# Two-block convolution and attention network, batch 4: another order at the start, image 2's and 3's normalisation in other banks, head attention through diagonal matrices

## What is computed

```python
x = x + L0(gn(x))     # block 1
x = x + L1(gn(x))     # block 2
# L0: the first 48 channels: layer norm over channels at each pixel, q (16), k (16), v (48),
#     full softmax attention over the 1024 pixels; relu(concat(attended, other 144)), a 192x192 product
# L1: qkv = 192 -> 576; heads of 24 channels: attention over channels of a head (q, k normalised
#     over the pixels, times a temperature, softmax over 24), attended = attn @ v
#     conv_x = depthwise 3x3 of a 1x1 of v;  t = cp_in(attended) (32 channels)
#     channel map from t, mean(t) and a 3x3 and a dilated 7x7 convolution of t
#     spatial map from conv_x: 1x1, depthwise 3x3, gelu gate, 1x1
#     out = proj(attended * sigmoid(spatial) + conv_x * sigmoid(mean of the channel map))
```

## Time and profile before

| what | value |
|---|---|
| median of 3 runs | 359.26 us (358.64 to 360.69) |
| the profiled execution | 360.42 us |
| its span, first to last instruction | 358.4 us |
| PE / DVE / ACT / POOL busy | 312.2 / 265.2 / 167.0 / 23.3 us |
| mean granted TensorE clock | 0.965 |

### The profile page before, as it was taken

How to read it: one execution, slowest core, us unless ns; L and a number is a source line. 1 busy time by engine, 2 the same in 40 slices (tenths; PEclk the granted TensorE clock), 3 DMA queues, 4 the chain that set the end, 5 groups by cost and what they waited for, 6 DMA issues and landing times. The chain is left out here.

```text
span 358.4 us, 6337 instructions
## 1 busy us (share of the span) xinstructions
PE 312.2 (87%) x2642; PEld 148.2 (41%) x2642; DVE 265.2 (74%) x496; ACT 167.0 (47%) x288; POOL 23.3 (6%) x29
## 2 busy tenths in 40 slices
PE   0279899999999599999899999998999878897995
PEld 0146265333346334543353546444243355433431
DVE  4444765867278957779989679978967999769653
ACT  1024307664561348734832387536632774375320
POOL 2012010000002400000100110001000001100000
PEclk9999758999999969999999999999999999999999
DMA  8460000000000000210000010200000315013005
GB/s 263 153 180 2 0 0 0 2 0 3 0 3 2 0 2 16 63 25 0 2 0 3 0 34 13 59 0 2 0 2 0 114 30 135 2 34 69 2 2 176
DMA packets 6074, 12.45 MB, mean 35 GB/s; under 512 B 2078, under 2 KB 2718, under 8 KB 5918
## 3 DMA queue, kind: packets, MB, share of 16 engines
q1 hardware_dynamic: 5532, 11.97, 12.3%
q10 hardware_dynamic: 514, 0.08, 0.1%
HBM read 5.32 MB, written 3.15 MB: 24 GB/s over the span
## 5 line engine op out<-in xcount | busy, mean ns | idle before, releaser
L1639 DVE SCALAR_TENSOR_TENSOR dd<-spp,wt,dd 112x1024 f32<-112x1024 f32 x32 | 41.0, 1283 | 2.5 <-ACT dd L2214 1.7
L1628 DVE SCALAR_TENSOR_TENSOR cx<-cpA,dw2w,cx 128x1024 f32<-128x1024 f32 x32 | 40.9, 1277 | 1.9 <-ACT cx L2133 1.8
L2101 ACT ACTIVATE pT<-psA 128x1024 f32<-128x1024 f32 x24 | 24.6, 1024 | 20.2 <-PE psA L649 15.1
L658 PE MATMUL psO<-pT,vt 128*64 128x512 f32 x96 | 25.1, 612 | 0.3 <-ACT pT L2101 0.2
L1628 DVE SCALAR_TENSOR_TENSOR cx<-cpB,dw2w,cx 128x512 f32<-128x512 f32 x32 | 23.8, 744 | 0.0
L1487 DVE TENSOR_REDUCE nmp<-psA 128x2 f32<-128x1024 f32 x16 | 19.6, 1225 | 5.3 <-PE psA L629 5.1
L845 PE MATMUL psR<-up,wb 128*32 128x256 f32 (+1 forms) x336 | 20.9, 383 | 0.1
L2059 ACT ACTIVATE xa<-x,gb,gr 48x512 f32<-48x512 f32 x8 | 6.5, 811 | 24.1 <-DVE gb L1444 24.0
L649 PE MATMUL psA<-qs,ks 50*128 50x512 f32 x48 | 12.0, 496 | 4.2 <-ACT pT L2101 2.6
L1419 DVE BATCH_NORM_STATS2 st<-x 128x6 f32<-128x512 f32 x24 | 15.5, 683 | 0.2
L2458 POOL TENSOR_TENSOR gr<-gvar,mhalf 128x2 f32<-128x2 f32 x8 | 6.0, 754 | 140.7 <-DVE gvar L1438 140.7
(11 more groups left out here) (429 smaller groups left out, 691.8 us busy)
## 6 DMA issues: line engine op xcount, KB each, us to landing
up<-up SPq DMA_DIRECT2D x12, 200.0 KB, 3.1
x<-x_dram SPq DMA_DIRECT2D x4, 512.0 KB, 6.0
out_dram<-x SPq DMA_DIRECT2D x8, 256.0 KB, 2.3
wt<-params_dram SPq DMA_DIRECT2D x1, 1151.5 KB, 6.8
tp<-tp SPq DMA_DIRECT2D x8, 136.0 KB, 2.4
x<-x_dram SPq DMA_DIRECT2D x8, 128.0 KB, 4.6
out_dram<-x SPq DMA_DIRECT2D x8, 128.0 KB, 2.5
wt<-params_dram SPq DMA_DIRECT2D x1, 213.5 KB, 2.6
```

Source lines behind the costliest of these rows:

```text
L658: last = mm(s.o_ps[rows(n), :], s.vt[:, t, :], s.pT[t % 2][:, n * HB:(n + 1) * HB], start=(t == 0), stop=(t == NKT - 1))
L1628: v.scalar_tensor_tensor(acc, img, dw2w[:, blk, tap:tap + 1], acc, ALU.mult, ALU.add).then_inc(cv_s.of(c), 1)
L1639: v.scalar_tensor_tensor(acc, t.spp[:, dy:dy + HH, dx:dx + WW], par("w_spdw")[:, tap:tap + 1], acc, ALU.mult, ALU.add).then_inc(dv_s.of(c), 1)
L2101: a(s.pT[t % 2][:], s.scoreT_ps[:], ACT.Exp).then_inc(ex_s.of(b), 1)
```

## The change

It does six things.

1. SP loads image 0 ahead of the first parameters; ACT issues its small loads first; DVE makes image 0's statistics before the group matrices are spread, and `setup2_a`, which waits for the small loads, stands behind `pixel_var(0)`. DVE norms one half of image 0's 48 channels itself (`normed1_half`), ACT the other.
2. PE begins with six products of `xn`, which POOL has filled with ones (`warm_up`), a seventh after `setup_ln`; the `keep_warm` products stand at other places.
3. The norm chains of images 2 and 3 use other banks (`cen_ps`, `norm_ps`, `mean_ps`: image 2 psR and psS, image 3 psB) and own semaphores and run ahead; `q_product`, `t_product(0)`, `sp_in_a(0)` and `conv1_a(2)` get waits for it. The inverse denominators get a tile of their own, `rD`.
4. Head scores are made transposed and copied (`copy_scores`), and multiplied by a diagonal of k's inverse norms on PE (`k_scaled`), which gives them scaled and the other way round; the mask is added in the same DVE instruction. The division by the softmax sums is a product with a diagonal too (`divided_attn`), which also transposes.
5. t's weights come from the undivided exponentials: `t_head` multiplies them by `wcpT` divided by the sums (`wcs`), `t_weights` by v's weights. The product of attention by v's weights and its 384-column copy go away.
6. All five lists are in another order; `store(0)` and `store(1)` stand ahead of `shift_u(1)` and `shift_t(2)`.

```diff
-        one[0].cen_ps, one[1].cen_ps = psR[:, 0:HB], psA[:, 0:HB]
+        cen_ps = [psR[:, 0:HB], psA[:, 0:HB], psR[:, 0:HB], psB[:, 0:HB]]
+        norm_ps = [psR[:, HB:N], psO, psR[:, HB:N], psB[:, HB:N]]
+        mean_ps = [psS, psO, psS, psB[:, HB:N]]
...
+            load_x(0)
             sp.dma_start(wt[:, 0:N1], params[:, 0:N1]).then_inc(s_w1, 16)
-            load_x(0)
             load_x(1)
...
             def group_means(i, b):
-                if i == 0 and TURN1[b]:
-                    pe.wait_ge(*x2_s(b - 1, 2))
-                    pe.wait_ge(*gmm[1](b - 1, 1))
+                if i == 0 and b == 2:
+                    pe.wait_ge(*x2_s(0, 2))
+                    pe.wait_ge(*gmm[1](0, 1))
+                if i == 0 and b == 3:
+                    pe.wait_ge(*mce_s(1, 3))
+                    pe.wait_ge(*mte_s(1, 4))
...
-            def k_norm_rows(c):
+            def k_scaled(c):
                 pe.wait_ge(*dk_s(c, 2))
+                pe.wait_ge(*rk_s(c, 1))
                 for h in range(2):
-                    for j in range(2):
-                        last = mm(front.F[1][rows(j), h * CH:(h + 1) * CH], ones[0:CH, 0:SP2], front.dk[:, h, :],
-                                  start=True, stop=True)
+                    last = columns(front.F[1][:, h * CH:(h + 1) * CH], front.st[:, h * CH:h * CH + P], front.dk[:, h, :])
...
+            def t_head(c):
+                pe.wait_ge(*sm_s(c, 6))
+                for h in range(2):
+                    last = columns(front.F[0][:, h * C6:(h + 1) * C6], front.sx[:, h * CH:h * CH + P], front.wcs[:, h, :])
+                last.then_inc(uh_s.of(c), 1)
...
             def attn_weights(c):
                 pe.wait_ge(*ate_s(c, 1))
                 wv = par2("wv")
                 for h in range(2):
-                    last = columns(front.F[0][:, h * C:(h + 1) * C], front.att[:, h * CH:h * CH + P], wv[:, h, :])
-                last.then_inc(mp_s.of(c), 1)
-                for h in range(2):
...
+            def warm_up(k):
+                if k == 0:
+                    pe.wait_ge(s_fill, 1)
+                mm(psB[:, HB:N][:, 0:QB], one[0].xn[:, 0:P], one[0].xn[:, 0:QB], start=True, stop=True)
...
+            def normed1_half():
+                s, g = one[0], stats[0][0]
+                dve.wait_ge(*gmm[0](0, 4))
+                dve.wait_ge(s_mem, 3)
+                v.tensor_scalar(s.xa[SP2:SPN, :], xs[0][0:PD, 1, :], g.gr[0:PD, 0:1], g.gb[0:PD, 0:1],
+                                ALU.mult, ALU.add).then_inc(s_xa0, 1)
...
             def scaled_scores(c):
-                dve.wait_ge(*rk_s(c, 1))
+                dve.wait_ge(*kr_s(c, 1))
                 dve.wait_ge(*sm_s(c, 1))
-                dve.wait_ge(*sc_s(c, 1))
                 for h in range(2):
-                    v.scalar_tensor_tensor(front.dk[:, h, :], front.F[0][0:CH, h * CH:(h + 1) * CH], front.rq[:, h:h + 1],
-                                           front.rk[:, h, :], ALU.mult, ALU.mult).then_inc(sm_s.of(c), 1)
+                    v.scalar_tensor_tensor(front.sc[:, h, :], front.F[1][0:CH, h * CH:(h + 1) * CH], front.rq[:, h:h + 1],
+                                           par("mask"), ALU.mult, ALU.add).then_inc(sm_s.of(c), 1)
                 dve.wait_ge(*sm_s(c, 3))
-                v.tensor_tensor(front.dk[:], front.dk[:], par("mask").unsqueeze(1).broadcast_to([CH, 2, CH]),
-                                ALU.add).then_inc(sm_s.of(c), 1)
```

More of the change, by code:

```diff
@@ L1045, in _ @@
             transpose_x(0, 0)
-            transpose_x(0, 1)
             proj1_a(1)
             proj1_b(1)
+            proj1_last(1)
+            center(2)
+            transpose_x(0, 1)
             transpose_x(0, 2)
-            proj1_last(1)
+            pixel_var(2)
             gram_x(0)
+            gram_w(0)
             group_means(1, 1)
-            group_means(0, 2)
-            gram_w(0)
-            center(2)
+            rstd_rows(2)
             head_scores(0)
-            pixel_var(2)
             norms(0)
-            rstd_rows(2)
-            k_norm_rows(0)
+            q_product(2)
+            k_product(2)
+            k_scaled(0)
             sp_in_a(0)
-            q_product(2)
-            transpose_attn(0)
-            k_product(2)
+            t_head(0)
+            divided_attn(0)
+            t_weights(0)
             attn_weights(0)
-            t_weights(0)
             v_product(2)
+            score_rows(2, 0)
+            t_product(0)
             conv1_a(1)
             conv1_b(1)
-            score_rows(2, 0)
-            t_product(0)
             score_rows(2, 1)
+            ci1_product(0)
             conv1_last(1)
+            transpose_x(1, 0)
             score_rows(2, 2)
-            transpose_x(1, 0)
-            ci1_product(0)
+            ci2a(0)
+            score_rows(2, 3)
             transpose_x(1, 1)
             transpose_x(1, 2)
-            score_rows(2, 3)
-            ci2a(0)
             score_rows(2, 4)
@@ L1130, in _ @@
             proj2_last(0)
+            center(3)
+            sp_in_a(1)
+            pixel_var(3)
+            t_product(1)
             group_means(1, 2)
-            attn_weights(1)
-            group_means(0, 3)
-            sp_in_a(1)
             sp_in_b(1)
-            t_weights(1)
-            center(3)
-            t_product(1)
-            pixel_var(3)
+            rstd_rows(3)
+            ci1_product(1)
+            q_product(3)
             conv1_a(2)
             conv1_b(2)
-            rstd_rows(3)
+            ci2a(1)
             conv1_last(2)
-            ci1_product(1)
             transpose_x(2, 0)
-            ci2a(1)
+            k_product(3)
             transpose_x(2, 1)
             transpose_x(2, 2)
-            q_product(3)
-            k_product(3)
+            v_product(3)
             gram_x(2)
-            v_product(3)
             score_rows(3, 0)
-            gram_w(2)
-            score_rows(3, 1)
             ci2b(1, 0)
             ci2b(1, 1)
-            score_rows(3, 2)
+            score_rows(3, 1)
             ci2b(1, 2)
             ci2b(1, 3)
+            score_rows(3, 2)
+            ci2b(1, 4)
             score_rows(3, 3)
-            ci2b(1, 4)
+            gram_w(2)
+            score_rows(3, 4)
             ci2b(1, 5)
-            score_rows(3, 4)
+            score_rows(3, 5)
             sp_out_a(1)
             ci2b(1, 6)
-            score_rows(3, 5)
+            score_rows(3, 6)
             sp_out_b(1)
             map_mean(1)
-            score_rows(3, 6)
+            score_rows(3, 7)
             attended_a(1)
-            score_rows(3, 7)
-            attended_b(1)
             max_rows(3)
@@ L1227, in _ @@
             ci2b(2, 4)
-            k_norm_rows(3)
+            sp_out_a(2)
+            k_scaled(3)
+            sp_out_b(2)
             ci2b(2, 5)
-            ci2b(2, 6)
-            sp_in_a(3)
-            transpose_attn(3)
-            attn_weights(3)
-            t_weights(3)
-            sp_out_a(2)
+            sp_in_a(3)
+            t_head(3)
+            divided_attn(3)
+            t_weights(3)
+            attn_weights(3)
+            ci2b(2, 6)
+            map_mean(2)
             t_product(3)
-            map_mean(2)
             sp_in_b(3)
             ci1_product(3)
-            sp_out_b(2)
             attended_a(2)
@@ L1676, in _ @@
             channel_stats(0, 0, 2)
+            setup_ln()
             moments(0, 0)
-            setup2_a()
-            group_stats(0, 0)
-            group_shift(0, 0)
-            setup_qkv()
-            channel_stats(0, 1, 0)
-            channel_stats(0, 1, 1)
-            setup_marks()
-            pixel_var(0)
-            channel_stats(0, 1, 2)
-            moments(0, 1)
+            group_matrices()
+            setup_marks()
+            group_stats(0, 0)
+            channel_stats(0, 1, 0)
+            group_shift(0, 0)
+            normed1_half()
+            channel_stats(0, 1, 1)
+            setup_qkv()
+            channel_stats(0, 1, 2)
+            pixel_var(0)
+            moments(0, 1)
+            setup2_a()
             setup_weights()
-            setup2_b()
             layer_norm(0)
@@ L1741, in _ @@
             normed(0)
+            moments(0, 2)
+            channel_stats(0, 3, 0)
+            channel_stats(0, 3, 1)
+            channel_stats(0, 3, 2)
             inverse_denominators(1)
+            group_stats(0, 2)
+            group_shift(0, 2)
             conv2(0, 0)
```

578 lines of the change are left out of this document (308 added, 270 removed).

## The result

The changed kernel takes 350.63 us (median of four, 349.89 to 352.18) against 359.98 for the kernel before in the same comparison: a ratio of 0.973, 95% interval 0.9679 to 0.9782. That is 9.4 us less; 17 were forecast. The profiled execution has a span of 347.8 us, before 358.4.

The account below looks back on a forecast made before the run. PE bounds 130 to 204 us, DVE 278 to 306; loose time lay at the start, in the scores and at 98 to 130. 11 + 0 + 5 + 1 + 0 = 17 off a 358.4 span; predicted time 342.5, range 336 to 348.

Parts of the forecast that it names:

- Step 1: Start up to image 0's q product: earlier image load, statistics and norms, mostly at the high clock; -11 us.
- What I had named as a sign of being wrong: At the start: `center(0)` is held by the warm products.
- Step 2: Image 0's scores, from q to first exponentials: same products at the same low clock; 0, from -7 to +4 us.
- Step 3: Image 2's norm chain, moved ahead of image 0's head attention: score rows start earlier; -5, from -1 to -7 us.
- Step 4: Image 3 and the middle: less PE work in head attention, possible wait of `conv1_a(2)`; -1, from -2 to +2 us.
- Step 5: The end: mask addition and a product leave the path, other work moves ahead, these cancel; 0, from -2 to +1 us.
- the middle gives little: Image 1's products ahead of the exponentials cost 4, clock falls at image 2, Step 3 gives 1: 350.5 us; chance 0.12.
- A clock that doesn't fall in the scores: Score stage: the clock stays high, 7 us more gained, 335.5 us; chance 0.08.
- The first rival: Clock stays low at the start, warm products hold `center(0)`, the start gives 5: 348.5 us; chance 0.18.

## Why the prediction was right, and where it was off

The direction was right; the drop was 9.4 us instead of 17. The time, 350.63, lies outside the forecast's own 336 to 348 and inside the wider range that takes in most rivals, 335 to 351.5, near its end. Steps 1 and 3 came out as summed; two others came out some 3 us worse each, one by the clock and one by waits, and both had been put at nothing. By its own steps:

**Step 1, the start, forecast -11: measured -11.1.** Statistics began at 4.47 (forecast 5 to 7 for their stretch), `center(0)` at 13.68 (13), q at 21.28 (20 to 22). Undoing the start costs the whole gain, which confirms it by a run of its own. The size is in part luck: six traces with this start have q at 19.78 to 22.92, which is 12.6 to 9.4 us before that of before. The course was not quite the one forecast. The clock dropped for 3.4 us from 10 on, ten warm instructions took 4.11 us instead of 2.6, and `center(0)` stood behind them 1.4 us after its tile was ready. What I had named as a sign of being wrong is there, at a size that earlier data made up for. Where the ten ran at the high level (2.4 us, in four runs, three of them with more products of ones) q comes at 19.7 to 20.4.

**Step 2, image 0's scores, forecast 0: measured +3.1 at the last exponentials of image 1.** This is one of the two mis-sized terms. I took the low stretch of before as fixed, 17 us, and asked only what order PE's products have in it. The first exponentials came 31.7 us behind q instead of 25.2, and the attention loop gave back 3.4 of these 6.5, as forecast; the other 3.1 are 6.9 us more at the low clock. The sign that I had named, low clock beyond 20 us in the first 100, came about (27.3 with the start's). The value lies within my -7 to +4. Why the clock stayed low longer is open: the run with the order of before has the 23.9 us too. The Trainium skill (TensorE: Matmul & The Clock Gate, Part 4) says that a product in transpose mode doesn't count as busy as others do, from which I took that products now ahead of the transposed maxima would bring the clock back earlier. The trace doesn't agree with that: it came back 23.9 us after its fall instead of 17.0, and only when the transposed maxima ran. It doesn't tell whether these run in the mode that the page means.

**Step 3, image 2's chain, forecast -5: measured -5.4** up to image 2's exponentials, some 2.3 of it clock, by the run that fills the wait in the kernel before. The size agrees by other shares than mine: I had 7 for the earlier place, less some clock that would stay low. The score rows of image 2 come 7.9 us earlier, counted from the last exponentials of image 1, the exponentials only 5.4; from q it is 4.8 instead of the 7 that I named as a sign, since the scores of images 0 and 1 take 3.1 longer.

**Step 4, the middle, forecast -1: measured +0.1.** `conv1_a(2)` didn't wait for image 3's chain.

**Step 5, the end, forecast 0, from -2 to +1: measured +2.7.** The second mis-sized term, and outside its range. I set edits against each other that don't meet: the mask's 0.35 and the product's 0.88 leave a chain that waits elsewhere, while `gelu_product(2)` (1.41) and a wait of 0.63 lengthen DVE's full list up to the scores, and `map_mean(2)` holds the t product another 1.0. The runs on the end confirm that the wait and `map_mean(2)` are places where time goes (1.6 us won up to the t product), and also that it could not simply be had. The share of the gelu products isn't shown: moving them only opened a wait.

Sum: -11.1 + 3.1 - 5.4 + 0.1 + 2.7 = -10.6 in the trace, where -17 was forecast.

**The rivals.** The time lies at that of "the middle gives little" (350.5), but not by its mechanism: the clock did not fall at image 2, and step 3 gave its 5. A loss of the size of its first half, 3.1 us where 4 was the price, came about in the scores, but not as the price of image 1's products ahead of the exponentials: the order of before has it too. That the time is met is chance. A clock that doesn't fall in the scores was priced at 7 us; the runs that force it give 5.3 to 6.7. The first rival came about in part: in the traces in which the ten warm instructions ran wholly or partly low (4.03 to 4.64 us), q is at 21.3 to 23.2 instead of 19.8, 1.5 to 3.4 us later and not 6.

## What to carry to other kernels

Read the granted clock beside the busy share: a stage that is 95% busy can be at half speed, and here each further us of that cost 0.4 to 0.7 in the scores. A product that only fills a wait can pay (2.0 us, 0.7 to 3.3, for four of them), and an instruction that looks misplaced may be the filler of a wait: move it only with a look at what its engine does in its stead. A change in several parts should be run in parts: here one part carried the whole result, and the others' gain and loss cancelled. And one trace of a start doesn't give its size: the same start put q anywhere within 3.1 us.

## What the runs showed of the hardware

- The clock was low over 22 us in which PE was busy 20.8 (changed kernel). It fell behind a wait of 1.26 us there, and in one run at 21.0, behind none over 0.61. With that one wait filled it fell 7.9 us behind q instead of 5.8 to 6.7 (six traces); with all of them filled it didn't fall in that stage, in three kernels.
- The same ten warm instructions ahead of `center(0)` took 2.4 us in four traces, 4.03 and 4.11 in two and 4.64 in five. All three occur among the six traces with the same start, so the list alone doesn't set it.
- By the profile the same operation on POOL, the inverse norms of image 3, took 1.00 us in five of the 14 traces, 1.57 in two and 1.98 to 2.10 in seven, with no difference of the kernels that goes with it.
